# Scan stage: step size from two ScalarE squares, output bias added to the residual by GpSimd

## The chip, the cores and the metric

The kernel runs on one core of one Trainium2 chip. The metric is the device time of one execution in microseconds, the median of several runs. Before the change three runs took 1969.9, 1974.85 and 1976.41 us.

## The reference, cut to what matters

The program is a four-layer network on an activation x of 4 x 512 tokens of 128 features. Each layer does `xn = layernorm(x)` and `x = x + attention(xn) + ffn(xn)`. The change touches only layer 2 (the third one), whose attention is a selective state-space scan and whose ffn is a mixture of 8 experts with top-2 routing:

```python
x_and_res = x @ in_proj_w.T + in_proj_b
x_in = silu(x_and_res[..., :128]); res = x_and_res[..., 128:]
ssm = x_in @ x_proj_w.T + x_proj_b                 # 16 + 128 + 128 columns
delta = clip(softplus(ssm[..., :16] @ dt_proj_w.T + dt_proj_b), 1e-05, 0.1)
Bm, Cm = ssm[..., 16:144], ssm[..., 144:]
A = clip(-exp(A_log), -5.0, -0.01)                 # 128 x 16
# per time step:
h = clip(h * clip(exp(A * delta), 1e-6, 1) + Bm * delta * x_in, -100, 100)
y = sum_over_16(h) * Cm + D_param * x_in
attention = (y * silu(res)) @ out_proj_w.T + out_proj_b
# ffn: hidden = silu(xn @ w_gate.T); sum over 8 experts of combine[:, e] * (hidden @ w_down[e].T)
```

`delta` is the step size. It is softplus of a linear form, clipped at 0.1, so only small values of `exp(z)` matter and `log(1 + exp(z))` can be a short polynomial.

## The kernel before, in words

The kernel runs the layers one after the other; between two blocks of code all engines meet at a barrier. Layer 2 is `norm_and_logits` (layer norm, transposes, router logits) and then `scan_and_ffn`, whose work lies from about 751.7 to 938 us of the trace. The residual x stays in SBUF as 16 tiles of 128 tokens by 128 features (four tiles for each of the four sequences; a sequence is called a batch b here). Small weights are loaded by SyncE's queue during the norm (L3136), among them `b_o`, the output bias, as one row of 4 x 128; every engine waits at the start of the scan block until all of these loads have landed.

The block has a preamble and a loop.

The preamble: TensorE projects the normed input (L1447) into four PSUM banks `m`, ScalarE applies Silu to them (L1554), and TensorE makes the inputs dt, B and C from x_in in one PSUM bank `x` (L1457). VectorE meanwhile does the router: a chain of small operations of 128x128 elements that picks the two best experts (`choose`, L1652 to L1656, L1786 to L1789). After it VectorE makes z, the argument of exp, from the dt bank (`size_input`, L1664), ScalarE exponentiates z in place (`exp_z`, L1568), and VectorE evaluates a polynomial of degree 7 in exp(z) (`log_terms`, L1673, L1676 and five times L1679), and clips it to `delta` (`step_size`, L1683). For batch 0 these steps lie between the steps of the running count of the experts (L1812). GpSimd makes `xd`, `cr`, `xp` and `dr` from delta, x_in and res (L1616 to L1625). ScalarE ends its preamble with the Silus of the other three batches, and then makes the 16 decays `da` of batch 0 (`decays`, L1574 and L1578).

The loop has 4 batches of 16 slots. In slot n of batch b VectorE does, in this order written out by hand: the scan of state n over 512 time steps (L1841), for b < 3 one step of the preparation of batch b+1 (`prepare_slot`), and two weighted sums of an expert's output into x (`weigh`, L1751). In the preparation, slot 1 holds `size_input` (for b+1 of 2 or more), slots 2 to 8 hold one of the seven operations of the polynomial each, slot 9 `step_size`, and slots 11 to 15 the input u of the next scans and a check of its size. Slot 3 also holds `mix` (L1767, y of the batch before from the summed states), and slot 10 `add_out` (L1775, the output product of the batch before added to x). Between two batches VectorE reads a flag and branches (`guard`).

TensorE adds up the 16 states of a batch in PSUM through products with the identity (L1531 and, for a correction, L1535), makes the experts' products four slots ahead (L1479), the next batch's inputs in slots 0, 2 and 5 (L1457), and after slot 6 `out_products`: the bias as a product of a row of ones with `b_o` (L1489, 1 by 512, which also opens the accumulation), four products of `dr` (L1493) and four of `y` (L1497). The last `out_products` stands behind the loop.

What ties the engines: a scan may be four ahead of TensorE's adding (four `h` buffers), four PSUM banks hold the experts' products, and ScalarE's decays have two sets of buffers. SyncE fills memory for layer 3 by DMA during the block.

Of the kernel before, what the change touches and what calls it, by code (L numbers as in the profile page):

```python
# [1315 lines left out]

LOG1P = (1.0, -0.49999995, 0.33332896, -0.24986669, 0.1980376, -0.15143938, 0.0804507)


def scan_tiles(nc, ctx, k, d):  # L1320

    k.s2 = {}
    sources = (("w_in", [P, 2 * P], "s2_w_in"), ("w_dl", [16, P], "s2_w_dl"), ("w_dt", [16, P], "s2_w_dt"),
               ("b_dl", [16, 1], "s2_b_dl"), ("b_dt", [P, 1], "s2_b_dt"), ("b_in", [P, 2], "s2_b_in"),
               ("wg", [P, 2, P], "f2_wg"), ("w_x", [P, 2 * P], "s2_w_bc"), ("b_bc", [P, 2], "s2_b_bc"),
               ("a_log", [P, 16], "s2_a_log"), ("dpar", [P, 1], "s2_dpar"), ("w_o", [P, P], "s2_w_o"),
               ("b_o", [1, 4, P], "s2_b_o"), ("wd", [P, 2, 8, P], "f2_wd"))
    for name, shape, _ in sources:
        k.s2[name] = ctx.enter_context(nc.sbuf_tensor(f"s2_{name}", shape, F32))
    loads = [(k.s2[name], d[src]) for name, _, src in sources]  # L1330
    return loads[:-1], loads[-1]


def scan_and_ffn(nc, k, tag, capacity, band, spare_rows):
# [21 lines left out]
    with ExitStack() as ctx:  # L1356
# [17 lines left out]
        z = ph.sb("z", [P, 2, T])  # L1374
        lp = ph.sb("lp", [P, T])
        delta = ph.sb("delta", [P, 2, T])
        xd = ph.sb("xd", [P, T])
# [26 lines left out]
            "mixed", "cr_ready", "dr_ready", "o_full", "o_read", "link", "size_ready", "top_ready", "table"))  # L1404
        xp_ready = ph.sem("xp_ready")
        lg = k.logits[:, 0:NT * E].rearrange("p (m e) -> p m e", e=E)
# [20 lines left out]
        def _(pe):  # L1427
# [56 lines left out]
            def out_products(b):  # L1484
                if b:
                    pe.wait_ge(o_read, b)
                else:
                    pe.wait_ge(routed, 1)
                pe.matmul(o_ps[:, :], k.ones[0:1, :], b_o[:, :, :].rearrange("a i d -> a (i d)"), start=True, stop=False,  # L1489
                          skip_group_check=True)  # L1490
                pe.wait_ge(dr_ready, b + 1)
                for i in range(QT):
                    pe.matmul(o_ps[:, i * P:(i + 1) * P], dr[:, b % 2, i * P:(i + 1) * P], w_o[:, :], start=False, stop=False,  # L1493
                              skip_group_check=True)
# [47 lines left out]
        def _(act):  # L1542
# [23 lines left out]
            def exp_z(b):  # L1566
                act.wait_ge(z_ready, b + 1)
                act.activation(z[:, b % 2, :], z[:, b % 2, :], ACT.Exp).then_inc(e_ready, 1)  # L1568

            def decays(b):  # L1570
                act.wait_ge(delta_ready, b + 1)
# [3 lines left out]
                for n in range(S):  # L1575
                    if b >= 2 and n == 0:
                        act.wait_ge(scanned, S * (b - 1))
                    act.activation(da[:, b % 2, n, :], delta[:, b % 2, :], ACT.Exp, scale=a[:, n:n + 1]).then_inc(da_ready, 1)  # L1578

# [6 lines left out]
            act.activation(weight[:, 1, :], weight[:, 1, :], ACT.Exp).then_inc(table, 1)  # L1586
            exp_z(0)
            exp_z(1)
            inputs(0)
# [6 lines left out]
            for b in range(1, B):  # L1596
                if b > 1:
                    exp_z(b)
                inputs(b)
                decays(b)  # L1600

        @block.gpsimd
        def _(pool):
            pool.memset(hole[:, :], 1e9).then_inc(hole_set, 1)
            pool.memset(blank[:, :], 0.0).then_inc(hole_set, 1)
            pool.memset(corr[:, 0, :], 0.0).then_inc(corr_zero, 1)
            pool.memset(corr[:, 1, :], 0.0).then_inc(corr_zero, 1)
            pool.wait_ge(k.s2_in, 16 * N_LOADS)
            for b in range(B):
                for name in (("res", b), ("xi", b)):  # L1610
# [20 lines left out]
        def _(v):  # L1631
# [26 lines left out]
            def size_input(b):  # L1658
# [3 lines left out]
                if b >= 2:  # L1662
                    v.wait_ge(delta_ready, b - 1)
                v.tensor_scalar(z[:, b % 2, :], x_ps[:, :], b_fold[:, 0:1], float(np.log(0.2)), ALU.add, ALU.min)\  # L1664
                    .then_inc(x_free, 1)
                v.wait_ge(x_free, i + 1)
                v.sem_inc(z_ready, 1)

            def log_terms(b, n):
                zb = z[:, b % 2, :]  # L1670
                if n == 2:
                    v.wait_ge(e_ready, b + 1)
                    chain(v.tensor_scalar(lp[:, :], zb, LOG1P[6], LOG1P[5], ALU.mult, ALU.add))  # L1673
                elif n == 3:
                    settle()
                    chain(v.tensor_tensor(lp[:, :], lp[:, :], zb, ALU.mult))  # L1676
                else:
                    settle()
                    chain(v.scalar_tensor_tensor(lp[:, :], lp[:, :], LOG1P[8 - n], zb, ALU.add, ALU.mult))  # L1679

# [26 lines left out]
            def prepare_slot(b, n):  # L1707
                if n == 1 and b >= 2:
                    size_input(b)
                if 2 <= n <= 8:  # L1710
                    log_terms(b, n)
                if n == 9:
                    step_size(b)
# [23 lines left out]

            latest = {}
            links = [0]

            def weigh(j):
                p, e = j // 4, j % 4
                for name in fills_of(p):
# [3 lines left out]
                    if e == 0:  # L1747
                        v.wait_ge(m_full[q % NB], q // NB + 1)
                    if tile in latest:
                        v.wait_ge(*latest[tile])  # L1750
                    ins = v.scalar_tensor_tensor(k.x[:, tile, :], m_ps[q % NB][:, e * P:(e + 1) * P],  # L1751
# [17 lines left out]
            def add_out(b):  # L1769
                v.wait_ge(o_full, b + 1)  # L1770
                for tile in range(b * QT, (b + 1) * QT):
                    if tile in latest:
                        v.wait_ge(*latest[tile])
                xs = k.x[:, b * QT:(b + 1) * QT, :]
# [20 lines left out]
            v.tensor_scalar(a[:, :], a[:, :], -1.0, -5.0, ALU.mult, ALU.max).then_inc(a_raw, 1)  # L1795
            log_terms(0, 2)
            v.wait_ge(a_raw, 2)
            v.tensor_scalar(a[:, :], a[:, :], -0.01, None, ALU.min).then_inc(a_raw, 1)
            log_terms(0, 3)
            v.wait_ge(a_raw, 3)  # L1800
            v.tensor_reduce(a_slow[:, :], a[:, :], AX.X, ALU.max).then_inc(a_raw, 1)
            log_terms(0, 4)
            v.wait_ge(both_ready, 1)
            total = v.tensor_copy(before[:, 0, :], both[:, 0, :])
            for i in range(1, NT - 1):
                chain(total)
                if i <= 4:
                    log_terms(0, 4 + i)
                if i == 5:
                    step_size(0)  # L1810
# [1337 lines left out]
def laid_out(a):  # L3148
# [45 lines left out]
    d["s2_w_dt"], d["s2_w_o"] = a["L2_attn_dt_proj_w"].T, a["L2_attn_out_proj_w"].T  # L3194
    d["s2_b_o"], d["s2_b_in"] = np.tile(a["L2_attn_out_proj_b"], (1, 4, 1)), col(a["L2_attn_in_proj_b"], 2)
    xb = a["L2_attn_x_proj_b"]
# [21 lines left out]
```

## Time and profile before

| | us |
|---|---|
| median of 3 runs (lowest, highest) | 1974.85 (1969.9, 1976.41) |
| the profiled execution: its time | 1978.25 |
| its span in the trace | 1976.4 |
| TensorE busy | 1804.1 (91%) |
| VectorE busy | 1469.5 (74%) |
| ScalarE busy | 967.7 (49%) |
| GpSimd busy | 905.5 (46%) |
| granted TensorE clock, mean | 0.951 of full |

The shares are averages over four layers with different limits. The change touches about 186 us of the span, so what counts is which engine sets the pace there. All times below are in us from the span's start; "busy" of TensorE counts overlapping instructions by their modelled ends.

### The profile page before, as it was taken

The numbers are of one execution on the slowest core, as the hardware profiler recorded it, in microseconds if no ns is written. First come the engines' busy times: TensorE is split into PE (matmuls) and PEld (weight loads), VectorE is DVE, ScalarE is ACT, GpSimd is POOL, SyncE is SP. The second block draws the span as 40 slices with busy tenths as digits, with TensorE's granted clock in tenths as the row PEclk, the third lists the DMA queues.
The fourth block names the chain that finished last, engine by engine and source line by source line (L and its number), as shares of the span: only waits on it lengthen the run. The fifth ranks groups of instructions, "written<-read, shape, count | busy, mean of one in ns | idle before, by whom it ended". The sixth has DMA issues, their size and how long they took to land. (4 is left out here: it accounts for less than half of the span.)

```text
span 1976.4 us, 32804 instructions
## 1 busy us (share of the span) xinstructions
PE 1804.1 (91%) x9914; PEld 999.3 (51%) x9914; DVE 1469.5 (74%) x4406; ACT 967.7 (49%) x2260; POOL 905.5 (46%) x1311
## 2 busy tenths in 40 slices
PE   6499997699989948898799999999999999999998
PEld 4233333455546634343466666644455555555544
DVE  6578886677757765998477678568877777777788
ACT  3258785376754426221577777733333333433332
POOL 1637772076633321111277777745444455433441
PEclk9579999699999977999899999999999999999999
DMA  8462223433451029950766566311311342423211
GB/s 285 138 137 33 39 31 65 99 78 106 83 159 29 21 70 160 178 127 0 187 184 166 151 168 182 86 63 46 96 62 62 120 138 84 139 83 102 63 33 33
DMA packets 240592, 201.92 MB, mean 102 GB/s; under 512 B 26883, under 2 KB 223016, under 8 KB 239782
## 3 DMA queue, kind: packets, MB, share of 16 engines
q1 hardware_dynamic: 222614, 171.43, 35.6%
q0 software_dynamic: 17376, 28.29, 5.6%
q8 instruction: 86, 1.41, 0.3%
q14 instruction: 84, 0.69, 0.1%
q10 hardware_dynamic: 432, 0.10, 0.0%
HBM read 116.87 MB, written 82.89 MB: 101 GB/s over the span
## 5 line engine op out<-in xcount | busy, mean ns | idle before, releaser
L2871 DVE SCALAR_TENSOR_TENSOR x<-f_m,f_gs,x 128x128 f32<-128x128 f32 x1024 | 304.8, 343 | 60.4 <-PE f_m L2696 52.9
L515 DVE TENSOR_REDUCE a_nmax<-a_s 128x1 f32<-128x512 f32 (+3 forms) x512 | 276.7, 585 | 83.2 <-PE a_s L321 36.5
L2238 POOL TENSOR_SCALAR a_lg<-a_lg,a_rinv 128x256 f32<-128x256 f32 (+1 forms) x256 | 226.3, 901 | 94.2 <-DVE a_rinv L2275 93.9
L2696 PE MATMUL f_m<-f_wo,f_oT 128*128 128x512 f32 x512 | 248.2, 595 | 0.9
L2644 POOL DMA_INDIRECT f_yg<-yslot,slot x160 | 152.5, 953 | 190.5 <-PE f_s L2730 106.7
L432 ACT ACTIVATE a_pT<-a_st 128x512 f32<-128x512 f32 (+3 forms) x512 | 227.6, 519 | 20.5 <-PE a_st L344 6.6
L318 PE MATMUL a_s<-t_kp,t_qp 96*128 96x512 bf16 (+3 forms) x512 | 166.5, 360 | 12.8 <-DVEq L499 12.6
L341 PE MATMUL a_st<-t_qp,t_kp 99*128 99x512 bf16 (+3 forms) x512 | 163.0, 353 | 2.0 <-ACT a_pT L432 1.2
L2696 PEld LDWEIGHTS f_m<-f_wo,f_oT 128*128 128x128 f32 x512 | 96.0, 190 | 125.6 <-issue 111.2
L2824 ACT COPY f_pT<-f_t 128x512 f32<-128x512 f32 x128 | 75.2, 588 | 167.4 <-PE f_t L2738 127.4
L2871 DVE SCALAR_TENSOR_TENSOR f_val<-f_m,gate,f_val 128x128 f32<-128x128 f32 x336 | 113.2, 343 | 39.7 <-PE f_m L2696 27.4
L2170 ACT ACTIVATE a_lg<-a_lg,a_nmax 128x256 f32<-128x256 f32 (+1 forms) x256 | 120.8, 475 | 31.5 <-DVE a_nmax L2268 31.4
L2730 PE MATMUL f_s<-xn_pair,f_qT 128*128 128x512 f32 x256 | 131.8, 596 | 0.0
L2634 POOL DMA_INDIRECT spare_rows<-xn_pair,slot x96 | 93.0, 969 | 78.5 <-PE f_s L2730 55.9
L442 ACT CAST t_qp<-a_m 3x512 bf16<-3x512 f32 x128 | 74.0, 578 | 102.8 <-PE a_m L329 95.4
L2915 DVE TENSOR_REDUCE f_nmax<-f_s 128x1 f32<-128x512 f32 x128 | 87.4, 683 | 42.5 <-PE f_s L2730 42.4
L2751 PE MATMUL f_o<-f_pT,f_val 128*128 128x512 f32 x256 | 115.2, 593 | 0.0
L2268 DVE CUSTOM_DVE_ANT_0 a_lg<-a_m,a_band 128x256 f32<-128x256 f32 (+1 forms) x256 | 85.0, 384 | 39.1 <-issue 31.9
L356 PE MATMUL a_o<-a_pT,t_vp 128*32 128x512 f32 (+3 forms) x1024 | 108.9, 521 | 0.4 <-DVE a_og L522 0.4
L2634 POOL DMA_INDIRECT rows<-xn_pair,slot x64 | 61.5, 961 | 82.5 <-PE f_s L2730 65.7
L480 POOL DMA_INDIRECT yacc<-a_yc,seat x64 | 85.2, 1332 | 11.2 <-issue 3.4
L2831 ACT ACTIVATE f_prob<-f_s,f_nmax 128x512 f32<-128x512 f32 x128 | 89.1, 696 | 0.8 <-DVE f_nmax L2915 0.5
(428 smaller groups left out, 3757.3 us busy)
## 6 DMA issues: line engine op xcount, KB each, us to landing
a_band<-band SPq DMA_DIRECT2D x64, 512.0 KB, 5.8
band<-s_hole SPq DMA_DIRECT2D x16, 1032.0 KB
band<-a_rows SPq DMA_DIRECT2D x64, 256.0 KB, 5.6
yslot<-f_ys SPq DMA_DIRECT2D x45, 256.0 KB
f_xs<-spare_rows SPq DMA_DIRECT2D x9, 832.0 KB
w_gate_up<-f_wgu_in SPq DMA_DIRECT2D x4, 1536.0 KB, 14.5
t_qp<-parts SPq DMA_DIRECT2D x192, 32.0 KB
t_kp<-parts SPq DMA_DIRECT2D x192, 32.0 KB
```

The costliest lines, as they stand in the source:

```text
L318: last = pe.matmul(ps[:, 0:n], qp[0:MR, h, qt * P:(qt + 1) * P], kp[0:MR, h, 0:n], start=True, stop=not causal)
L341: last = pe.matmul(out[:, q0:T], kp[0:KT, i % H, kt * P:(kt + 1) * P], qp[0:KT, i % H, q0:T], start=True, stop=not causal)
L432: act.activation(pT[:, g % 2, i % 4, begins[kt]:begins[kt] + T - q0], st_ps[w % R][:, q0:T], ACT.Exp).then_inc(exp_done, 1)
L515: v.tensor_reduce(nmax[:, h % 4, qt:qt + 1], s_ps[(b * H * QT + u) % R][:, 0:n], AX.X, ALU.max, negate=True)\
L2170: last = act.activation(lg[:, g % 2, half, p, c0:c0 + w], lg[:, g % 2, half, p, c0:c0 + w], ACT.Exp, bias=nmax[:, g % 2, p, qt:qt + 1], sc ...
L2238: last = pool.tensor_scalar(lg[:, g % 2, half, p, c0:c0 + n], lg[:, g % 2, half, p, c0:c0 + n], rinv[:, g % 2, p, qt:qt + 1], None, ALU.mult)
L2634: pool.indirect_dma_start(rows[n % 3], place_of(c, i, h), k.xn[:, i, :], None).then_inc(sent[n % 3], 16)
L2644: pool.indirect_dma_start(yg[:, n % 2, c, i, :], None, yslot[nth(h) % 3], place_of(c, b * QT + i, h))\
L2696: pe.matmul(ps[:, :], left, w, start=True, stop=True).then_inc(full, 1)
L2730: pe.matmul(s_ps[u % 2][:, :], qT[:, g % 2, qt * P:(qt + 1) * P], tokens(g), start=True, stop=True).then_inc(s_done, 1)
L2751: last = pe.matmul(o_ps[:, :], val[:, g % 3, kt, :], pT[:, g % 2, kt, :], start=(kt == 0), stop=(kt == QT - 1))
L2871: ins = v.scalar_tensor_tensor(out, ps[:, e * P:(e + 1) * P], gate, out, ALU.mult, ALU.add)
```

## The change

The polynomial is written another way. With e = exp(z), before:

```python
LOG1P = (1.0, -0.49999995, 0.33332896, -0.24986669, 0.1980376, -0.15143938, 0.0804507)
```

After, ScalarE makes two shifted squares of e, and VectorE multiplies: lp = (square0 + r0) * e, then (square1 + r1) * lp, a degree 5 polynomial. The cap of z goes from log(0.2) to log(0.106).

The bias is loaded as 128 x 128 (one row for every partition), GpSimd adds it to the residual tiles in four operations of 128x512 at the start of the block, and TensorE's bias product goes. The first write of each x tile waits for that addition.

```diff
+LOG_SCALE = 0.6339928554569843
+LOG_SHIFT = (0.3520040145240758, -0.8358345770896863)
+LOG_REST = (0.8024751436592323, 0.3808488880994126)
...
-               ("b_o", [1, 4, P], "s2_b_o"), ("wd", [P, 2, 8, P], "f2_wd"))
+               ("b_o", [P, P], "s2_b_o"), ("wd", [P, 2, 8, P], "f2_wd"))
...
-                pe.matmul(o_ps[:, :], k.ones[0:1, :], b_o[:, :, :].rearrange("a i d -> a (i d)"), start=True, stop=False,
-                          skip_group_check=True)
                 pe.wait_ge(dr_ready, b + 1)
...
+            def squares(b):
+                if b:
+                    act.wait_ge(delta_ready, b)
+                else:
+                    act.wait_ge(shift_set, 2)
+                act.wait_ge(e_ready, b + 1)
+                for i in range(2):
+                    act.activation(square[:, i, :], z[:, b % 2, :], ACT.Square, bias=shift[:, i:i + 1], scale=LOG_SCALE)\
+                        .then_inc(squared, 1)
...
+                    if b == 0 and n == S // 2:
+                        squares(1)
...
             exp_z(0)
+            squares(0)
             exp_z(1)
...
                     exp_z(b)
+                    squares(b)
...
+            for i in range(2):
+                pool.memset(shift[:, i:i + 1], LOG_SHIFT[i]).then_inc(shift_set, 1)
...
             pool.wait_ge(k.s2_in, 16 * N_LOADS)
+            for b in range(B):
+                xs = k.x[:, b * QT:(b + 1) * QT, :]
+                pool.tensor_tensor(xs, xs, bc(b_o[:, :].unsqueeze(1), [P, QT, P]), ALU.add).then_inc(x_biased, 1)
...
-            def log_terms(b, n):
+            def log_term(b, i):
                 zb = z[:, b % 2, :]
...
+                v.wait_ge(squared, 2 * b + i + 1)
+                if i:
                     settle()
+                chain(v.scalar_tensor_tensor(lp[:, :], square[:, i, :], LOG_REST[i], lp[:, :] if i else zb, ALU.add, ALU.mult))
...
-                if 2 <= n <= 8:
-                    log_terms(b, n)
-                if n == 9:
+                if n in (4, 6):
+                    log_term(b, n // 2 - 2)
+                if n == 8:
                     step_size(b)
...
-            latest = {}
+            latest = {tile: (x_biased, tile // QT + 1) for tile in range(NT)}
```

In the preamble VectorE's seven polynomial operations for batch 0 become two, placed behind the second operation on `a` and in the first step of the running count; `step_size(0)` moves from step 5 of the count to step 3.

## Rows read from the trace of the kernel before

**Rows 1.** Busy time by stretch; columns: us, engines' busy us, TensorE clock, DMA share, GB/s.
```profile
863.50:884.70 21.20, 18.99 (x55) 8.51 (x54) 21.03 (x34) 2.01 (x3) 5.76 (x4) 1.00 0.02 5
823.00:844.20 21.20, 20.75 (x57) 9.43 (x56) 21.05 (x33) 2.01 (x3) 5.76 (x4) 0.95 1.24 182
903.00:933.00 30.00, 28.98 (x78) 12.62 (x76) 28.45 (x50) 0.00 (x0) 5.78 (x3) 1.00 0.00 1
820.00:825.00 5.00, 4.50 (x7) 1.65 (x6) 3.98 (x10) 0.00 (x0) 0.00 (x0) 0.67 1.27 159
```
**Rows 2.** Who waited for whom in the loop, 787 to 938 us.
```profile
DVE s_h L1841 <- PE s_sum L1531: 1.7, 2, 1.0
```
**Rows 3.** The same view in the first half of batch 2, 863.5 to 884.7 us.
```profile
PE s_sum L1531 <- DVE s_h L1841: 2.2, 1, 2.2
```
**Rows 4.** Timeline of VectorE in batch 1: start, duration, line, operation, tiles.
```profile
828.39 0.40 DVE L1673 TENSOR_SCALAR s_lp<-s_z 128x512 f32<-128x512 f32 x1
828.70 0.60 DVE L1751 SCALAR_TENSOR_TENSOR x<-s_m,s_gate,x 128x128 f32<-128x128 f32 x2
...
839.78 0.66 DVE L1679 SCALAR_TENSOR_TENSOR s_lp<-s_lp,s_z 128x512 f32<-128x512 f32 x1
840.37 0.60 DVE L1751 SCALAR_TENSOR_TENSOR x<-s_m,s_gate,x 128x128 f32<-128x128 f32 x2
```
**Rows 5.** Timeline of VectorE where GpSimd is at work, batch 1 and batch 3.
```profile
833.18 1.70 DVE L1679 SCALAR_TENSOR_TENSOR s_lp<-s_lp,s_z 128x512 f32<-128x512 f32 x1
...
836.46 1.75 DVE L1679 SCALAR_TENSOR_TENSOR s_lp<-s_lp,s_z 128x512 f32<-128x512 f32 x1
...
915.80 1.75 DVE L1841 TENSOR_TENSOR_SCAN s_h<-s_da,s_u 128x512 f32<-128x512 f32 x1
917.98 1.21 DVE L1841 TENSOR_TENSOR_SCAN s_h<-s_da,s_u 128x512 f32<-128x512 f32 x1
```
**Rows 6.** Timeline of GpSimd in batches 1 and 3.
```profile
832.28 2.05 POOL L1620 TENSOR_TENSOR s_cr<-s_cm,s_res 128x512 f32<-128x512 f32 x1 [23.44 <-DVE s_y L1767]
...
836.39 1.27 POOL L1625 TENSOR_TENSOR s_dr<-s_xp,s_res 128x512 f32<-128x512 f32 x1
...
915.20 1.27 POOL L1625 TENSOR_TENSOR s_dr<-s_xp,s_res 128x512 f32<-128x512 f32 x1
```
**Rows 7.** Timeline of TensorE and of VectorE at the end of the block.
```profile
933.17 1.12 PE L1489 MATMUL s_o<-s_b_o,ones 1*128 1x512 f32 x2
934.22 1.16 PE L1493 MATMUL s_o<-s_w_o,s_dr 128*128 128x128 f32 x8
...
933.28 0.69 DVE L1767 TENSOR_TENSOR s_y<-s_sum,s_cr 128x512 f32<-128x512 f32 x1 [1.57 <-PE s_sum L1535]
```
**Rows 8.** Timeline of VectorE in the preamble.
```profile
756.94 0.17 DVE L1789 TENSOR_TENSOR s_weight<-s_best 128x16 f32<-128x16 f32 x1
760.27 0.75 DVE L1664 TENSOR_SCALAR s_z<-s_x,s_b_fold 128x512 f32<-128x512 f32 x1 [3.16 <-PE s_x L1457]
...
781.71 1.23 DVE L1697 TENSOR_TENSOR_SCAN s_s<-s_da_slow,s_s 128x512 f32<-128x512 f32 x1 [4.48 <-ACT s_da_slow L1574]
```
**Rows 9.** Timeline of ScalarE in the preamble.
```profile
760.04 1.28 ACT L1583 ACT_TABLE_LOAD   x1
...
763.22 0.63 ACT L1568 ACTIVATE s_z<-s_z 128x512 f32<-128x512 f32 x1 [0.85 <-DVEq L1667]
764.98 0.69 ACT L1560 ACTIVATE s_bm<-s_x,s_b_bc 128x512 f32<-128x512 f32 x1 [1.12 <-PE s_x L1457]
```
**Rows 10.** GpSimd and VectorE in the preamble: the last clearing, then a product and what runs beside it.
```profile
752.52 0.52 POOL L1607 MEMSET s_corr<- 128x512 f32 x1
769.85 1.26 POOL L1616 TENSOR_TENSOR s_xd<-s_delta,s_xi 128x512 f32<-128x512 f32 x1 [16.81 <-DVE s_delta L1683]
...
769.97 1.16 DVE L1812 TENSOR_TENSOR s_before<-s_before,s_both 128x8 bf16<-128x8 bf16 x1
```
**Rows 11.** Timeline of SyncE's queue, the load of the bias row.
```profile
738.88 0.29 SPq L3136 DMA_DIRECT2D s_b_o<-s_b_o_in  x1
```

More of the change, by code:

```diff
@@ L1314, in _ @@
             v.wait_ge(weighed, 2 * NT)
-LOG1P = (1.0, -0.49999995, 0.33332896, -0.24986669, 0.1980376, -0.15143938, 0.0804507)
+LOG_SCALE = 0.6339928554569843
+LOG_SHIFT = (0.3520040145240758, -0.8358345770896863)
+LOG_REST = (0.8024751436592323, 0.3808488880994126)
 def scan_tiles(nc, ctx, k, d):
@@ L1326, in scan_tiles @@
                ("a_log", [P, 16], "s2_a_log"), ("dpar", [P, 1], "s2_dpar"), ("w_o", [P, P], "s2_w_o"),
-               ("b_o", [1, 4, P], "s2_b_o"), ("wd", [P, 2, 8, P], "f2_wd"))
+               ("b_o", [P, P], "s2_b_o"), ("wd", [P, 2, 8, P], "f2_wd"))
     for name, shape, _ in sources:
         k.s2[name] = ctx.enter_context(nc.sbuf_tensor(f"s2_{name}", shape, F32))
-    loads = [(k.s2[name], d[src]) for name, _, src in sources]
+    loads = [(k.s2[name], bc(d[src], [P, P]) if name == "b_o" else d[src]) for name, _, src in sources]
     return loads[:-1], loads[-1]
@@ L1375, in scan_and_ffn @@
         lp = ph.sb("lp", [P, T])
+        square = ph.sb("square", [P, 2, T])
+        shift = ph.sb("shift", [P, 2])
         delta = ph.sb("delta", [P, 2, T])
@@ L1404, in scan_and_ffn @@
             "mixed", "cr_ready", "dr_ready", "o_full", "o_read", "link", "size_ready", "top_ready", "table"))
-        xp_ready = ph.sem("xp_ready")
+        xp_ready, shift_set, squared, x_biased = (ph.sem(s) for s in ("xp_ready", "shift_set", "squared", "x_biased"))
         lg = k.logits[:, 0:NT * E].rearrange("p (m e) -> p m e", e=E)
@@ L1488, in out_products @@
                     pe.wait_ge(routed, 1)
-                pe.matmul(o_ps[:, :], k.ones[0:1, :], b_o[:, :, :].rearrange("a i d -> a (i d)"), start=True, stop=False,
-                          skip_group_check=True)
                 pe.wait_ge(dr_ready, b + 1)
                 for i in range(QT):
-                    pe.matmul(o_ps[:, i * P:(i + 1) * P], dr[:, b % 2, i * P:(i + 1) * P], w_o[:, :], start=False, stop=False,
-                              skip_group_check=True)
+                    pe.matmul(o_ps[:, i * P:(i + 1) * P], dr[:, b % 2, i * P:(i + 1) * P], w_o[:, :], start=(i == 0),
+                              stop=False, skip_group_check=True)
                 pe.wait_ge(mixed, b + 1)
@@ L1663, in size_input @@
                     v.wait_ge(delta_ready, b - 1)
-                v.tensor_scalar(z[:, b % 2, :], x_ps[:, :], b_fold[:, 0:1], float(np.log(0.2)), ALU.add, ALU.min)\
+                v.tensor_scalar(z[:, b % 2, :], x_ps[:, :], b_fold[:, 0:1], float(np.log(0.106)), ALU.add, ALU.min)\
                     .then_inc(x_free, 1)
@@ L1667, in size_input @@
                 v.sem_inc(z_ready, 1)
-            def log_terms(b, n):
+            def log_term(b, i):
                 zb = z[:, b % 2, :]
[L1671 to L1674, printed above, removed]
+                v.wait_ge(squared, 2 * b + i + 1)
+                if i:
                     settle()
[L1676 to L1679, printed above, removed]
+                chain(v.scalar_tensor_tensor(lp[:, :], square[:, i, :], LOG_REST[i], lp[:, :] if i else zb, ALU.add, ALU.mult))
             def step_size(b):
@@ L1748, in weigh @@
                         v.wait_ge(m_full[q % NB], q // NB + 1)
-                    if tile in latest:
-                        v.wait_ge(*latest[tile])
+                    v.wait_ge(*latest[tile])
                     ins = v.scalar_tensor_tensor(k.x[:, tile, :], m_ps[q % NB][:, e * P:(e + 1) * P],
@@ L1771, in add_out @@
                 for tile in range(b * QT, (b + 1) * QT):
-                    if tile in latest:
-                        v.wait_ge(*latest[tile])
+                    v.wait_ge(*latest[tile])
                 xs = k.x[:, b * QT:(b + 1) * QT, :]
@@ L1795, in _ @@
             v.tensor_scalar(a[:, :], a[:, :], -1.0, -5.0, ALU.mult, ALU.max).then_inc(a_raw, 1)
-            log_terms(0, 2)
             v.wait_ge(a_raw, 2)
             v.tensor_scalar(a[:, :], a[:, :], -0.01, None, ALU.min).then_inc(a_raw, 1)
-            log_terms(0, 3)
+            log_term(0, 0)
             v.wait_ge(a_raw, 3)
             v.tensor_reduce(a_slow[:, :], a[:, :], AX.X, ALU.max).then_inc(a_raw, 1)
-            log_terms(0, 4)
             v.wait_ge(both_ready, 1)
@@ L1806, in _ @@
                 chain(total)
-                if i <= 4:
-                    log_terms(0, 4 + i)
-                if i == 5:
+                if i == 1:
+                    log_term(0, 1)
+                if i == 3:
                     step_size(0)
@@ L3194, in laid_out @@
     d["s2_w_dt"], d["s2_w_o"] = a["L2_attn_dt_proj_w"].T, a["L2_attn_out_proj_w"].T
-    d["s2_b_o"], d["s2_b_in"] = np.tile(a["L2_attn_out_proj_b"], (1, 4, 1)), col(a["L2_attn_in_proj_b"], 2)
+    d["s2_b_o"], d["s2_b_in"] = a["L2_attn_out_proj_b"][None], col(a["L2_attn_in_proj_b"], 2)
     xb = a["L2_attn_x_proj_b"]
```

## The prediction

> **What bounds the kernel now.** First I read busy time by stretch inside the block that the change touches. In the loop VectorE has no idle time: 21.03 of 21.20 us in the first half of batch 2, 21.05 of 21.20 in the first half of batch 1 [rows 1]. TensorE is close behind it (18.99 and 20.75 of the same 21.20 us), so the next question is which of the two waits for the other. In the whole loop VectorE's scans waited for TensorE's adding twice, 1.7 us in all [rows 2], and both times at the change of a batch, beside the branch. TensorE in turn sat idle for a scan, 2.2 us at one place in the first half of batch 2 alone [rows 3]. So VectorE sets the pace of the loop, and an operation taken from its list shortens the loop by the time from its start to the start of the next one, not by its printed duration, since neighbours overlap.
>
> The preamble is another matter. VectorE idles 3.16 us before its first z, for TensorE, and 4.48 us before the size check, for ScalarE [rows 8]. The path there goes from z through TensorE's products and ScalarE's Silus to the decays; VectorE's polynomial lies beside it.
>
> Everything behind the block starts at a barrier, so what the block gains the kernel gains.
>
> **The loop.** Start to start, L1673 costs 828.70 - 828.39 = 0.31, and L1679 costs 840.37 - 839.78 = 0.59 [rows 4]; L1676 is like it, with the same inputs, so six are of that kind. Seven operations go: 0.31 + 6 x 0.59 = 3.85. Two come, of the form of L1679 with both inputs in SBUF as before: 1.18. `step_size` only moves. Saved: 2.67 a batch. The preparation of batches 1, 2 and 3 lies in the loop: 3 x 2.67 = 8.0 us.
>
> **The stalls beside GpSimd.** Two of the five L1679 take 1.70 and 1.75 in place of 0.66 [rows 5]; they start while GpSimd's `cr` (832.28 to 834.33) and `dr` (836.39 to 837.66) run [rows 6]. These stalls of 1.04 and 1.09 are no property of the polynomial: they fall on what stands there. After the change slot 4 still holds such an operation, and `cr` still starts right behind `mix`: 1.04 stays. In slot 5 the operation is gone, and `dr` will meet the scan of slot 5 or 6. The row for that is in batch 3, where no polynomial runs: a scan started 0.6 us behind `dr` took 1.75 against 1.21, 0.54 more [rows 5, 6]. So 1.09 becomes 0.54, twice (batches 1 and 2): 1.1 us saved. Bounds: nothing saved, or all four stalls gone, 2 x (1.04 + 1.09) = 4.3. I take the batch 3 row, being the same pair of engines at the same distance.
>
> **The bias product.** It starts at 933.17 and the next product at 934.22 [rows 7]: 1.05 us. In the last `out_products` it runs while VectorE makes y, which ends at 933.28 + 0.69 = 933.97. Without it the four `dr` products end at 933.17 + 1.0 = 934.2, behind y, so the y products and the last addition come 1.05 earlier. The other three lie in the loop beside VectorE: nothing on the path, but 1.05 of relief for TensorE in each first half. `dr` must be there earlier now; behind `mix` it comes 5.6 us later (837.66), while TensorE reaches it only after the adding of slot 6, some 6 us behind `mix` at the earliest. If it should wait, the experts' products and the next adding queue behind it, and the four `h` buffers cover that.
>
> **ScalarE.** Two squares of 128x512 a batch: exp without bias took 0.63, Identity with a bias operand 0.69 [rows 9], so 1.3 for a pair, between 1.2 and 1.4. In the loop ScalarE works 2.01 us in the first 21.2 of a batch [rows 1], and z comes in slot 1 against the use of its square in slot 4: hidden. `squares(1)` stands in the middle of the decays of batch 0 and delays eight decays by 1.3; they are made at 0.62 apart from 781.5 on and used 1.6 and more apart from 787 on: hidden. In the preamble `squares(0)` stands ahead of `exp_z(1)`: exp of batch 0 ends about 762.4, the squares at 763.7, so `exp_z(1)` starts at 763.7 instead of 763.22 and ends at 764.3. Next is the B input at 764.98, which waits for TensorE [rows 9]: 0.65 us of cover are left. VectorE's five saved operations in the preamble are worth nothing, since 4.48 us of idle time already stand behind them [rows 8].
>
> **GpSimd's four additions.** This is the only part that can cost. They start when the clearing ends, 752.52 + 0.52 = 753.04 [rows 10], and two small ones more: about 753.3. One takes 1.26 when undisturbed, as a product of the same shape [rows 10], and 2.05 when disturbed [rows 6]. They run beside the router chain of 13 steps, 0.32 apart, which ends at 756.94 + 0.17 = 757.11 [rows 8]; most of its steps have two SBUF inputs. The rows show what that does: beside `xd` (769.85 to 771.11) a step of the count, also with two SBUF inputs and far smaller, took 1.16, to 771.13 [rows 10]. So each addition lets about one such step through. Four of them run to 753.3 + 4 x 1.26 = 758.3; the chain has got through four blocked steps and one free one by then and has seven left at 0.32 each: 758.3 + 2.3 + 0.15 = 760.8. The first z was due at 760.27 [rows 8]. The 3.16 us of idle time absorb most, and the path slips by 0.5 us. Ends: nothing, if GpSimd is the one that waits; with 2.05 each, 753.3 + 8.2 + 2.45 = 763.95, 3.7 us late. I take 0.5, since the rows at 769.85 have the same engine and the same kind of step.
>
> The Trainium skill ("SBUF — State Buffer", Who interferes with whom) says that a VectorE instruction with two SBUF inputs and a GpSimd instruction that reads SBUF exclude each other, the later one blocking fully until the first is done. The blocked step of 1.16 us agrees [rows 10], and the rule speaks against this change; by it every addition blocks the chain for its whole length, 4 x 1.26 = 5.0 on top of 757.11, thus 762.2 and 1.9 late, which would make the sum 1.4 us smaller. The stretched L1679 of 1.70 agree less: `cr` was stretched too.
>
> **The load.** The bias is now 64 KB in place of 2 KB, issued at 738.88 [rows 11], 12.8 us before the block; it must land by 751.7. Nothing on the path. The first weighing in slot 0 waits for `x_biased`, 758.3 against 788: done.
>
> **The sum.** 8.0 + 1.1 + 1.05 - 0.5 = 9.65 us. The profiled execution took 1978.25 and would take 1968.6; it lay 3.4 above the median of the runs. From the median: 1974.85 - 9.65 = 1965.2.
>
> **The rivals.**
> - *TensorE takes over in the first halves* (chance 0.12). The half of batch 2 shrinks from 21.2 to 21.2 - 2.67 - 0.55 = 18.0. TensorE's work there is 18.99 - 1.05 = 17.9, in batch 1 20.75 - 1.05 = 19.7 [rows 1]. If its 2.2 us of idle time [rows 3] can't be filled, it needs 20.1, twice, and 1.7 more in batch 1 for the low clock: 2 x 2.1 + 1.7 = 5.9 lost, 3.7 gained, 1971.1. Against it: in batch 3 TensorE is busy 28.98 of 30 us [rows 1] and no scan waits, as the buffers reach four slots ahead; and the second halves are loose.
> - *GpSimd's additions run at 2.05* (0.09): slip 3.7 in place of 0.5, gain 6.45, 1968.4.
> - *Square needs a table of its own* (0.05). A load is 1.28 [rows 9]; ahead of the squares and behind them, `exp_z(1)` ends at 764.3 + 2.56 = 766.9, 1.9 behind 764.98. Gain 7.75, 1967.1. In the loop the loads are hidden. Identity follows exp without a load in the trace; Square is not in it. The Trainium skill ("ScalarE: Activation LUTs", Table sets: the hidden batching unit) names cheap functions that are in every set, without Square among them.
> - *The change doesn't reach the total* (0.05): behind the block TensorE sets the pace, and two more dips of its clock there, each like the 5 us at 0.67 from 820 on [rows 1], cost 2 x 2.5: 1970.2.
> - *Slower, by TensorE's clock* (0.05). The granted clock is 0.67 from 820 to 825 [rows 1], when TensorE has been waiting for scans at the end of batch 0, and it is back by 825. While it is at 1.2 GHz instead of 2.4 its work doubles. A dip of d us puts TensorE d/2 behind; some 3 us of buffers cover that. So it costs d/2 - 3, eats the gain from d = 25 us on, and makes the kernel slower by 0.3% from d = 37 on. With 40 us, one batch: 1965.2 + 17 = 1982. Against it: the one dip is under 5 us, and TensorE's gaps get shorter, not longer.
>
> **How the numbers follow.** The forecast has 0.64. Its own range, with the bounds of the stalls and of the slip and the spread of the runs (5 us below the median, 1.6 above), is 1960 to 1968.5. To leave out no more than 0.2 the range goes up to the first rival: 1960.0 to 1971.2. A measurement tells about 0.3%, 5.9 us, from no change, so faster means below 1968.9. The forecast gives 0.61 of its 0.64 to that, GpSimd's slowness 0.05 of 0.09, the table 0.04, TensorE's takeover 0.03: 0.73. Slower is 0.05. The rest is 0.22.
>
> **What would show it.** Right: batches of the loop 3.2 us shorter (40.4 to about 37.2 from the first scan of batch 1 to that of batch 2), no scan waiting for TensorE in slots 4 to 8, VectorE's first z at 760.8, the last y products straight behind `mix`. Wrong: VectorE's waits for TensorE above 1.7 us, a table load beside the squares, a first loop scan later than 788, additions longer than 1.3, or a clock below 1 beyond 825. If the block is shorter by 9 to 10 us and the total is not, the cause lies behind the block.

## The result and the profile after

The changed kernel takes 1962.31 us (median of 14 runs, 1956.99 to 1969.7); the kernel before, on the same chip, 1974.86 (1969.19 to 1977.49). The ratio is 0.9944, 95% interval 0.9933 to 0.9954, that is 9.1 to 13.2 us faster, 11.1 in the middle. 1965.2 was forecast, with a gain of 9.65.

The profiled execution of the changed kernel took 1956.99 us, 21.3 less than that of before. To say where this comes from I cut both traces at the same marks: VectorE's first instruction of the block, the first scan of each batch, the last y (`mix`), the last `add_out`, and the first statistics of layer 3. "Batch" below is from its first scan to that of the next, less the idle time at the branch between them.

| stretch, us | before | changed |
|---|---|---|
| ahead of the block (no edit there but the size of one load) | 751.77 | 743.79 |
| preamble, to the first scan | 35.45 | 33.11 |
| batches 0, 1, 2 | 34.78, 39.10, 39.00 | 32.03, 35.72, 35.73 |
| the three branches | 0.98, 1.44, 0.74 | 1.35, 0.78, 0.44 |
| batch 3, to the last y | 30.02 | 30.03 |
| last y to its addition | 3.03 | 1.94 |
| addition to layer 3 | 2.00 | 2.01 |
| the block | 186.54 | 173.14 |
| layer 3 | 1038.1 | 1037.9 |

So the block is 13.4 us shorter, and 8.0 of the 21.3 lie ahead of it, in code that differs only in the size of the bias load. The block's own difference is what has to be explained.

Busy time of the changed kernel by stretch: the two halves of batch 2, and batch 3; columns as in [rows 1].

```profile
846.80:865.30 18.50, 18.50 (x56) 9.07 (x55) 18.35 (x30) 3.34 (x5) 5.76 (x4) 1.00 0.48 140
865.30:882.90 17.60, 14.93 (x35) 5.87 (x34) 17.14 (x32) 10.52 (x17) 1.28 (x1) 1.00 0.00 0
882.95:912.90 29.95, 28.43 (x78) 12.78 (x77) 28.45 (x50) 0.00 (x0) 5.77 (x3) 1.00 0.00 1
```

VectorE has no idle time in the first half still (18.35 of 18.50), and TensorE, which had 2.2 us [rows 1], has none left either (17.9 busy of 18.0 were forecast). This view can't tell which one holds the other up. The view of who waited for whom in the loop says more; it answers to [rows 2]:

```profile
PE s_sum L1534 <- DVE s_h L1854: 10.1, 14, 1.4
DVE s_h L1854 <- PE s_sum L1534: 2.6, 3, 1.3
DVE x L1790 <- PE s_o L1500: 1.2, 1, 1.2
```

VectorE's three waits, 2.6 us, all stand at the three branches; no scan inside a batch waits. That the view names TensorE there means only that its adding ended last: the scan behind the third branch, at 882.95, needs the buffer of the scan four before it, and TensorE had finished with that by 878.44. So the idle time is that of reading the flag and branching, and it is 3.2 us at the same three places in the kernel before. TensorE still waits for scans, 10.1 us in all.

Timeline of VectorE in batch 1 of the changed kernel, where GpSimd's work meets it, and of GpSimd there (this answers to [rows 4 to 6]):

```profile
818.31 1.22 DVE L1854 TENSOR_TENSOR_SCAN s_h<-s_da,s_u 128x512 f32<-128x512 f32 x1
819.44 1.69 DVE L1696 SCALAR_TENSOR_TENSOR s_lp<-s_square,s_z 128x512 f32<-128x512 f32 x1
821.05 0.60 DVE L1767 SCALAR_TENSOR_TENSOR x<-s_m,s_gate,x 128x128 f32<-128x128 f32 x2
821.57 1.21 DVE L1854 TENSOR_TENSOR_SCAN s_h<-s_da,s_u 128x512 f32<-128x512 f32 x1
822.70 0.58 DVE L1767 SCALAR_TENSOR_TENSOR x<-s_m,s_gate,x 128x128 f32<-128x128 f32 x2
823.20 1.78 DVE L1854 TENSOR_TENSOR_SCAN s_h<-s_da,s_u 128x512 f32<-128x512 f32 x1
824.91 0.66 DVE L1696 SCALAR_TENSOR_TENSOR s_lp<-s_square,s_lp 128x512 f32<-128x512 f32 x1
```

```profile
818.54 2.04 POOL L1642 TENSOR_TENSOR s_cr<-s_cm,s_res 128x512 f32<-128x512 f32 x1 [24.39 <-DVE s_y L1783]
820.56 2.00 POOL L1643 TENSOR_SCALAR s_xp<-s_xi,s_dpar 128x512 f32<-128x512 f32 x1
822.64 1.27 POOL L1647 TENSOR_TENSOR s_dr<-s_xp,s_res 128x512 f32<-128x512 f32 x1
```

The first polynomial operation meets `cr` and takes 1.69 as before; the second is past `dr` and takes 0.66; in its place the scan of slot 6, started 0.56 behind `dr`, takes 1.78 in place of 1.21.

TensorE and VectorE at the end of the block; this answers to [rows 7]. The bias product is gone, and the y products start at 913.72, behind the last `dr` product and right behind y (912.98 + 0.69 = 913.67):

```profile
912.78 1.05 PE L1496 MATMUL s_o<-s_w_o,s_dr 128*128 128x128 f32 x8
913.72 1.16 PE L1500 MATMUL s_o<-s_w_o,s_y 128*128 128x128 f32 x8
...
912.98 0.69 DVE L1783 TENSOR_TENSOR s_y<-s_sum,s_cr 128x512 f32<-128x512 f32 x1 [1.57 <-PE s_sum L1538]
914.92 0.69 DVE L1790 TENSOR_TENSOR x<-s_o,x 128x512 f32<-128x512 f32 x1 [1.25 <-PE s_o L1500]
```

The preamble, GpSimd's additions and the router chain beside them (this answers to [rows 8, 10]), and ScalarE's squares with what follows ([rows 9]):

```profile
745.06 5.09 POOL L1630 TENSOR_TENSOR x<-x,s_b_o 128x512 f32<-128x512 f32 x4
...
745.39 1.08 DVE L1675 TENSOR_TENSOR s_below<-logits,s_best 128x128 f32<-128x128 f32 x1
746.51 1.24 DVE L1676 SCALAR_TENSOR_TENSOR s_below<-s_below,iota 128x128 f32<-128x128 f32 x1
747.78 0.29 DVE L1677 TENSOR_REDUCE s_where<-s_below 128x16 f32<-128x128 f32 x1
748.11 0.92 DVE L1678 TENSOR_TENSOR s_first<-iota,s_where 128x128 f32<-128x128 f32 x1
749.06 1.24 DVE L1801 TENSOR_TENSOR s_ex<-logits,s_best 128x128 f32<-128x128 f32 x1
750.33 0.29 DVE L1802 SCALAR_TENSOR_TENSOR s_left<-s_first,logits 128x128 f32<-128x128 f32 x1
...
752.28 0.17 DVE L1804 TENSOR_TENSOR s_weight<-s_best 128x16 f32<-128x16 f32 x1
753.15 0.75 DVE L1686 TENSOR_SCALAR s_z<-s_x,s_b_fold 128x512 f32<-128x512 f32 x1 [0.69 <-PE s_x L1462]
```

```profile
755.35 1.33 ACT L1580 ACTIVATE s_square<-s_z,s_shift 128x512 f32<-128x512 f32 x2
756.59 0.61 ACT L1571 ACTIVATE s_z<-s_z 128x512 f32<-128x512 f32 x1
757.29 0.69 ACT L1563 ACTIVATE s_bm<-s_x,s_b_bc 128x512 f32<-128x512 f32 x1
```

Four steps of the chain stretch to 0.92 to 1.24, one for each addition; the step that only reads one SBUF tile (L1677) passes at 0.29 beside them, and the chain ends 8.66 us into the block in place of 5.34. No table load stands beside the squares. Yet the first scan comes earlier than before, which no step of the forecast gives. That is the question for the experiments.

### The profile page after: what moved, and what is told of

It is laid out like the page before. It is cut to its first block and busy times, and to the rows that moved or that the text cites. A ratio compares the mean times of both kernels' runs of the same rounds, so it can differ in the third digit from the quotient of the medians.

```text
span 1954.8 us, 32809 instructions
## 1 busy us (share of the span) xinstructions
PE 1788.0 (91%) x9906; PEld 995.1 (51%) x9906; DVE 1460.5 (75%) x4386; ACT 971.4 (50%) x2268; POOL 911.2 (47%) x1317
```

## The experiments

All ratios are against the kernel before on the same chip.

### Which part brings what: e1 and e2

e1 is the changed kernel with TensorE's bias product back and GpSimd's additions gone; e2 is the kernel before with the bias part alone.

```diff
 # e1, against the changed kernel
+                pe.matmul(o_ps[:, :], k.ones[0:1, :], b_o[:, :, :].rearrange("a i d -> a (i d)"), start=True, stop=False,
+                          skip_group_check=True)
...
-                pool.tensor_tensor(xs, xs, bc(b_o[:, :].unsqueeze(1), [P, QT, P]), ALU.add).then_inc(x_biased, 1)
```

> The change without its bias part: the squares and the short polynomial stay, the output bias goes back to TensorE as a product of ones. Block is counted from VectorE's first instruction to the first statistics of layer 3: 186.5 us before, 173.1 changed. My theory (the loop is VectorE's): loop shorter by 9.1 to 10.0 as in the changed kernel, tail not shorter (y to its addition 3.0 us, not 1.9), router chain undisturbed (4.0 us, not 7.3), preamble to the first scan 35.4 if the low TensorE clock near the 10th us of the block belongs to the kernel before, 33 or less if the high clock comes with ScalarE's squares; block 175 to 177.5, total 8.5 to 11.5 faster than before. Rival (the preamble's 2.3 us come from the bias part): preamble 35.4 here and 33.1 in the bias part alone.

> The bias part alone: the polynomial of seven VectorE operations stays. My theory: tail 1.05 shorter; loop unchanged within 0.5 us, since VectorE keeps its list and TensorE's three products less in the loop free nothing; router chain 3.3 longer as in the changed kernel, with a slip of 0.3 to 0.9 of the first z; total 0 to 1 faster, not distinguishable from before. Rival (TensorE also held the loop): the loop shrinks by 1 us or more. Rival (the preamble's 2.3 us come from the bias part): preamble 33.1 and total 3 faster.

e1: 0.994 (0.9919 to 0.9961), so 7.7 to 16.0 us faster. e2: 1.0006 (0.9991 to 1.0021). The time is the polynomial's. In e1 the batches are 32.02, 35.78 and 35.73, as in the changed kernel, and y to addition is 3.03; in e2 they are 34.78, 38.98 and 38.98, as before, and y to addition is 1.94. So taking three bias products from TensorE in the loop frees nothing, and the one in the tail is worth 1.09. Both preambles are long, 35.05 and 35.50. The rival, that the bias part shortened the preamble, falls; and e1 has the squares, so they did not do it either. In e2 the first z waits for the router chain, where in the kernel before it waited for TensorE [rows 8]:

```profile
758.98 0.17 DVE L1790 TENSOR_TENSOR s_weight<-s_best 128x16 f32<-128x16 f32 x1
759.38 0.75 DVE L1665 TENSOR_SCALAR s_z<-s_x,s_b_fold 128x512 f32<-128x512 f32 x1 [0.23 <-DVE s_weight L1790]
```

That is 8.85 us into its block (750.53), against 8.50 before and 8.41 in e1: a slip of 0.35 to 0.44 (0.63 against e3's 8.22, below).

### Where the additions cost: e3 and e7

e3 holds the additions until both z are made. e7 puts four more GpSimd products of the same size between them, on data that nothing uses.

```diff
 # e3
             pool.wait_ge(k.s2_in, 16 * N_LOADS)
+            pool.wait_ge(z_ready, 2)
 # e7
+                pool.wait_ge(extra, b)
+                pool.tensor_tensor(cr[:, :], k.xnT[:, 0:T], k.xnT[:, T:2 * T], ALU.mult).then_inc(extra, 1)
```

> The changed kernel with GpSimd's four additions held until both z are made. My theory: the router chain takes 4.0 us again; the first z stands at 8.5 from the block's start if TensorE is at full clock by then, so 0.3 to 0.9 us against the changed kernel at the most, and the additions meet the running count, which lies beside ScalarE's Silus and costs nothing; total equal to the changed kernel within 1 us. Rival (the additions cost their 3.3 us on the path): 2 us or more faster than the changed kernel.

> The changed kernel with four more GpSimd products of 128x512 between the four additions, on data that nothing uses, so GpSimd works 10.2 us beside the router chain in place of 5.1. My theory (each operation lets about one two-input step of the chain through, and there are only 9 of these in the chain): the chain ends 3 to 4 us later, at about 12 from the block's start in place of 8.7, the cover is used up, and the first z and the first scan stand 3 to 3.5 later; total 3 us slower than the changed kernel. Rival (the cover is deeper, since ScalarE's Silus set the preamble): first scan at most 1 us later.

e3: 0.9942 (0.9919 to 0.9964), not to be told from the changed kernel. Its chain ends at 5.34 again, z stands at 8.22, the first scan at 34.86.

e7: 0.998 (0.9965 to 0.9995), some 7 us slower than the changed kernel, where 3 were expected. The chain ends at 11.79, forecast 12; z slips to 12.02. Eight of its steps are now blocked, one for each operation of GpSimd; three of them, with a step between that passes:

```profile
759.87 1.24 DVE L1806 SCALAR_TENSOR_TENSOR s_left<-s_first,logits 128x128 f32<-128x128 f32 x1
761.14 0.29 DVE L1678 TENSOR_REDUCE s_best<-s_left 128x16 f32<-128x128 f32 x1
761.46 0.92 DVE L1679 TENSOR_TENSOR s_below<-s_left,s_best 128x128 f32<-128x128 f32 x1
762.41 1.24 DVE L1680 SCALAR_TENSOR_TENSOR s_below<-s_below,iota 128x128 f32<-128x128 f32 x1
...
764.95 0.17 DVE L1808 TENSOR_TENSOR s_weight<-s_best 128x16 f32<-128x16 f32 x1
765.35 0.75 DVE L1690 TENSOR_SCALAR s_z<-s_x,s_b_fold 128x512 f32<-128x512 f32 x1 [0.23 <-DVE s_weight L1808]
768.41 0.75 DVE L1690 TENSOR_SCALAR s_z<-s_x,s_b_fold 128x512 f32<-128x512 f32 x1 [2.31 <-PE s_x L1463]
```

The first scan stands at 40.71. Against e4, which has the changed preamble and the same behaviour of the clock (below), 3.1 us of slip in the first z became 4.1 in the second and 5.1 in the first scan, because TensorE worked at 1.2 GHz for longer: its product behind the first z took 2.05 in place of 1.10, and the clock was back at 2.4 GHz only 24 us into the block, in e4 at 18. I had 3 to 3.5. So the cover is about 2.9 us: the 3.16 of idle time less the 0.22 that stand between the chain and z in any case. Four additions lengthen the chain by 3.32, which is 0.4 more than that.

### Does VectorE still set the pace: e4

The second of the two polynomial operations is left out in the loop, so part of the step size of batches 1 to 3 isn't computed (the other one waits for both squares).

```diff
-                if n in (4, 6):
-                    log_term(b, n // 2 - 2)
+                if n == 4:
+                    log_term(b, 0)
```

> The changed kernel with the second of the two polynomial operations left out for batches 1, 2 and 3, so that part of the step size is not computed. My theory (VectorE still sets the pace): 0.59 less in each of three batches, 1.8 us less in the loop than the changed kernel. Rival (TensorE has taken over in the first halves): loop shorter by under 0.6 in all, scans waiting for TensorE's adding in slots 4 to 8.

Batches 31.43, 35.23 and 35.12: 0.60, 0.49 and 0.61 below the changed kernel, 1.7 us in all against 1.8 expected. In the view of waits, VectorE's scans have two waits put down to TensorE's adding, both at branches:

```profile
PE s_sum L1534 <- DVE s_h L1854: 8.5, 13, 1.4
DVE s_h L1854 <- PE s_sum L1534: 1.2, 2, 0.8
```

TensorE has not taken over, though it is busy through the whole first half. The total, 0.9948 (0.9929 to 0.9967), is too coarse to show 1.7 us.

### On what the stall behind mix falls: e6

The two operations move to slots 3 and 7, off the place right behind `mix`.

```diff
-                if n in (4, 6):
-                    log_term(b, n // 2 - 2)
+                if n in (3, 7):
+                    log_term(b, (n - 3) // 4)
```

> The changed kernel with the two polynomial operations in slots 3 and 7 in place of 4 and 6, so that none stands right behind mix, where GpSimd's cr starts. My theory (the stall of 1.0 us falls on the two-input operation that meets cr; a scan that meets GpSimd loses 0.5): batches 1 and 2 show the pattern of batch 3, stalls of 0.5 and 0.5 in place of 1.0 and 0.6, so 0.5 us less in each, 1 us in all. Rival (GpSimd holds VectorE up for as long whatever stands there): batches 1 and 2 as long as in the changed kernel, 36.5 and 36.2.

Batches 32.03, 35.17 and 35.17: 0.55 and 0.56 less in batches 1 and 2. The stalls are now those of batch 3 in the kernel before [rows 5]; the timeline of batch 2, from the polynomial operation in slot 3 on:

```profile
861.36 0.67 DVE L1696 SCALAR_TENSOR_TENSOR s_lp<-s_square,s_z 128x512 f32<-128x512 f32 x1
...
862.47 0.68 DVE L1783 TENSOR_TENSOR s_y<-s_sum,s_cr 128x512 f32<-128x512 f32 x1
863.06 1.21 DVE L1854 TENSOR_TENSOR_SCAN s_h<-s_da,s_u 128x512 f32<-128x512 f32 x1
...
864.70 1.72 DVE L1854 TENSOR_TENSOR_SCAN s_h<-s_da,s_u 128x512 f32<-128x512 f32 x1
...
868.48 1.74 DVE L1854 TENSOR_TENSOR_SCAN s_h<-s_da,s_u 128x512 f32<-128x512 f32 x1
```

The total, 0.9949 (0.9934 to 0.9965), can't show 1.1 us.

Not tried by an edit, but to be read from these traces, is what sets the size of a stall. It is not the kind of instruction: in slot 9 of the changed kernel a scan meets `xd` and loses 0.87, more than any scan beside `cr` or `dr`:

```profile
829.34 1.27 POOL L1638 TENSOR_TENSOR s_xd<-s_delta,s_xi 128x512 f32<-128x512 f32 x1 [4.97 <-DVE s_delta L1700]
829.61 2.08 DVE L1854 TENSOR_TENSOR_SCAN s_h<-s_da,s_u 128x512 f32<-128x512 f32 x1
```

When it starts, `xd` still has 1.00 to run. The same count gives: polynomial operation at 819.44, `cr` has 1.14 left, 1.03 lost; scan at 823.20, `dr` has 0.71 left, 0.57 lost; e6's scans at 864.70 and 868.48, 0.64 and 0.66 left, 0.51 and 0.53 lost. The loss is each time the time that GpSimd's product still has to run, less 0.11 to 0.15. So e6 gains because the next instruction with two SBUF inputs stands 0.5 further behind the start of `cr`, not because it is a scan. Beside `xp`, a `TENSOR_SCALAR` of GpSimd, the scan at 821.57 took 1.21 as ever, and `xp` itself 2.00 in place of the 1.57 that it takes in the preamble.

### The preamble: e5, e9 and e10

The granted clock of TensorE, by stretch, tells the preambles apart. The rows are 5 to 6 us, 6 to 8 us (left out for before, which has 1.00 from 6 us on) and 12 to 18 us into the block; first the kernel before, then the changed one.

```profile
756.77:757.77 1.00, 1.00 (x3) 0.38 (x2) 0.31 (x2) 0.79 (x3) 0.00 (x0) 0.96 1.26 183
763.77:769.77 6.00, 5.13 (x7) 1.85 (x6) 5.66 (x16) 2.63 (x4) 0.00 (x0) 0.50 1.26 182
```

```profile
748.79:749.79 1.00, 1.00 (x2) 0.34 (x1) 0.97 (x2) 0.63 (x2) 1.00 (x2) 0.50 1.47 157
749.79:751.79 2.00, 2.00 (x5) 0.91 (x4) 1.83 (x6) 1.04 (x2) 0.36 (x1) 0.80 1.24 194
755.79:761.79 6.00, 4.76 (x11) 2.08 (x12) 5.50 (x15) 4.60 (x7) 2.47 (x2) 1.00 1.35 180
```

Before, the clock rises to 2.4 GHz near 5 us and is back at 1.2 GHz from 12 to 18 us; in the changed kernel's profile it rises only near 7 us and then stays. Behind the rise TensorE makes single products and waits about 1 us ahead of each (1.01, 1.01 and 0.87 in the kernel before). e5 fills those waits in the changed kernel, e9 in the kernel before, with products whose result is unused, the first of them 8.35 us into the block in e5, behind the rise; e10 is the changed kernel unaltered.

```diff
+                if 1 <= turn[name] <= 3:
+                    pe.matmul(sum_ps[1][:, 0:384], k.ident[:, :], k.xnT[:, 0:384], start=True, stop=True)
                 if turn[name]:
                     pe.wait_ge(x_free, turn[name])
```

> The changed kernel with three idle-time products added on TensorE in the preamble (identity by 384 columns, each ahead of the wait for the x bank, result unused). In five of six profiles so far TensorE's clock rose to 2.4 GHz about 5 us into the block and was at 1.2 GHz again from about 12 to 18.5 us; in the changed kernel's own profile it rose at 7 us and stayed. My theory: that fall belongs to TensorE's gaps around the two z, not to the change. With the gaps filled the clock stays up after its rise, the first loop scan stands at 33.5 or less from the block's start in place of 34.9 to 35.6, and the median is 1.5 to 2.5 us below the changed kernel's. Rival (the fall comes at its own time, whatever TensorE does): clock at 0.5 near the 12th to 18th us again, first scan at 35 or later.

> The kernel before with the three idle-time products of e5 added on TensorE in the preamble, and nothing else. My theory (the fall of TensorE's clock at 12 us into the block belongs to TensorE's gaps, the change has no part in it): the clock stays up after its rise, the first loop scan stands at 33 in place of 35.0 to 35.5, the rest of the block is as in the kernel before: batches of 35.2 to 35.8, 40.0 to 40.5 and 39.7. Total some 2 us below before, near the limit of what can be told. Rival (the change itself holds the clock up, with its squares or additions): clock at 0.5 near the 12th us, first scan at 35.

> The changed kernel once more, unaltered, for another look at the preamble and for its time beside e11 on the same chip. If the clock's rise near 5 us leads to the fall at 12: first scan at 35 to 35.6, block 175 to 175.5; if it rises near 7 us: 33.1 and 173.1. Loop in either case 136.1 from the first scan to the last y, 1.94 from y to its addition. If the preamble of the first profile belonged to the change, it comes out at 33.1 whatever the clock did.

| rise of the clock | kernels | clock at 12 to 18 us | first scan at |
|---|---|---|---|
| early, waits unfilled | before, e1, e2, e3, e4 (e7 apart) | 1.2 GHz | 34.9 to 35.6 |
| late, waits unfilled | changed, e6, e10 | 2.4 GHz | 33.1 to 33.5 |
| late, filled | e9 | 2.4 GHz | 32.9 |
| early, filled | e5, e8, e11 | 2.4 GHz | 32.9, 32.0, 32.0 |

The row that decides is e5's, where the clock rises early (0.92 from 5 to 6 us) and stays:

```profile
756.64:757.64 1.00, 1.00 (x3) 0.38 (x2) 0.97 (x2) 0.74 (x3) 1.00 (x2) 0.92 1.26 160
...
763.64:769.64 6.00, 5.87 (x14) 2.42 (x14) 5.58 (x16) 4.44 (x8) 2.92 (x3) 1.00 1.29 139
```

So the fall belongs to the unfilled waits together with an early rise. Up to the first scan it costs 2.2 to 2.9 us (e4 against the changed kernel's three late rises and e5; e3 against e8; before against e9). e4 has the changed kernel's preamble and fell; so the change doesn't prevent it. And e9 is the kernel before and rose late, ahead of its first added product; so the late rise doesn't need the change, and e9 shows nothing of the filling.

Whether the change makes the late rise likelier stays open: with its preamble (the profiles of after, e4, e5, e6 and e10) the clock rose late in three of five, in the other preambles in one of eight.

The totals of e5, 0.9947 (0.9929 to 0.9965), of e9, 0.9994 (0.998 to 1.0008), and of e10, 0.9948 (0.993 to 0.9967), bear out no gain of 2 us from filling, where e5 was expected 1.5 to 2.5 us below the changed kernel and e9 2 us below the kernel before: where the late rise comes by itself there is less to win, and the runs of each spread over 8 to 13 us.

### All three together: e8 and e11

e8 has e3's wait, e5's products and e6's slots; e11 is the same kernel once more.

> The changed kernel with the additions held until both z are made, the three idle-time products of e5, and the polynomial in slots 3 and 7. If all three theories hold: first z at 8.3, no fall of the clock, first scan at 32.7, batches 1 and 2 0.5 shorter each; 3 to 3.5 us below the changed kernel. If only the loop part holds: 1 us below.

> The kernel of e8 once more. Its block was 170.9 us, 2.2 shorter than the changed kernel's, yet its layer 3 took 1043.5 us against 1037.9, and the total showed no gain. Theory one: layer 3 varies by some 5 us from execution to execution whatever stands ahead of it; then its layer 3 comes out elsewhere between 1038 and 1043 and the median is 1 to 3 us below the changed kernel's. Theory two: what e8 does makes layer 3 longer; then it is at 1043 again and the totals are equal.

The block takes 170.91 and 170.56 us, against 173.14 and 173.25 (e10): 2.2 and 2.7 less: 1.0 to 1.1 from the slots, 1.1 and 1.4 from the preamble, the rest at the branches. The totals: e8 0.9954 (0.9938 to 0.9971); e11 0.9937 (0.9921 to 0.9953) beside e10's 0.9948 on the same chip, medians 1957.55 (e11) and 1960.16 (e10). For e8 3 to 3.5 us below the changed kernel were expected; its total shows none of it. This kernel beats the kernel before; that it beats the changed one shows in the block and isn't settled in the total. Layer 3 took 1043.5 us in e8 and 1037.6 in e11, with the same kernel, so its length varies by itself; nothing shows that e8's came from the edits.

## Why the prediction was right, and where it was off

- **VectorE sets the pace of the loop: right, and shown.** e4 moved the batches by 0.5 to 0.6 for one operation less, and e2 took three products from TensorE for nothing. The rival of TensorE's takeover fell.
- **2.67 us a batch: right, mis-sized by 0.08.** Batch 0, where no stall changes, is 2.75 shorter.
- **The stalls, 0.55 for batches 1 and 2: right in size.** Forecast 3.22 a batch; 3.27 in batch 2, 3.38 in batch 1 of the profile, 3.26 and 3.25 against e2's 38.98. The 1.09 became 0.57, and e6 turned the other 1.04 into 0.5. The row of batch 3 gave the right price because it had the same distance behind `dr` (0.60 against 0.56), as the prediction said; the same pair of engines would not have been enough, as the scan beside `xd` shows with 0.87.
- **The bias product, 1.05: right (1.09),** and nothing in the loop, by e2.
- **GpSimd's additions, 0.5 late: right where the clock rises early.** The first z was forecast at 760.8 - 751.77 = 9.0 into the block and came at 8.85 to 8.89 in e2, e4 and e5, with the chain ending at 8.62 to 8.66. Where the clock rises late, TensorE is itself 0.9 late (first z at 9.3 to 9.5, in e9 without any addition at 9.35) and the additions cost nothing. The upper end, 2.05 an addition, didn't occur: four took 5.09. The Trainium skill's rule ("SBUF — State Buffer", Who interferes with whom), read as the chain losing the whole length of every addition, put the end of the chain at 762.2, 10.4 us into the block; it came at 8.66. The trace agrees with the rule for the single blocked step: the router step at 746.51 met an addition that ran until 747.60 and ended at 747.75. But a step is blocked only for what is left of the addition when it starts: the four lose 0.79, 0.95, 0.63 and 0.95 over their usual 0.29, and these sum to the 3.32 by which the chain is longer, not to 5.1.
- **The squares hidden, no table load: right.** A pair takes 1.33. In the changed kernel's profile `exp_z(1)` ends at 757.20, the product of the B input at 756.15 + 1.10 = 757.25, and the B input starts at 757.29: of the cover of 0.65 next to nothing is left there. In e1, where the clock rose early as in the kernel before, 0.73 is left, and the B input starts 13.2 us into the block in both.
- **Missed: the branches.** They were left at what they were. The third takes 0.74 to 0.78 in all three kernels with the long polynomial and 0.41 to 0.45 in the ten profiles with a short one, 0.3 less. The first two scatter between 0.43 and 1.44, and e10 shows 1.06 at the first where the same kernel had 1.35. Why the third is shorter wasn't tried. The prediction also took the distance from the first scan of batch 1 to that of batch 2 as 40.4; it is 40.54 in the trace, and 36.50 in the changed kernel against the 37.2 given as a sign.
- **Missed in the profile: the preamble.** The forecast had 0.5 more, the profile 2.3 less. The step that failed is that the preamble of one execution was taken for the kernel's: which way the clock goes in it is worth 2 to 3 us. In this profile it happened to go the good way, and that is luck: 2.3 of the block's 13.4 us.
- **Two signs of being wrong that came up and meant nothing.** VectorE's waits put down to TensorE are 2.6 us, above the 1.7 named; they are the branches, whose idle time fell from 3.2 to 2.6. Additions longer than 1.3 us: three took 1.31 to 1.32.
- **TensorE's clock as a danger in the loop: rightly held small.** In the changed kernel's loop the clock is at 1.2 GHz once, for some 3.4 us about the change from batch 0 to batch 1, as before. In e9 it was there for 6.8 us in batch 2, and that batch still took 38.99.

Sum with what the runs show: 2.75 + 3.26 + 3.26 + 0.3 + 1.09 - 0.4 = 10.3, in the measured 9.1 to 13.2, whose middle is 11.1; the forecast said 9.65. What the late rise adds on average isn't known.

## What to carry to other kernels

Where one engine runs without a gap, count an edit start to start on that engine's own timeline, and put a stall next to another engine down to the place, not to the instruction: it passes on to whatever two-input instruction stands there next, and its size here was the time that the other engine's product still had to run. Before moving work to GpSimd beside a VectorE chain with two SBUF inputs, compare the idle time at the end of the chain with one GpSimd duration for each operation as an upper bound (here 0.63 to 0.95 of 1.27 to 1.32 each). And compare two profiles by stretches with the same marks: here 8 of 21 us of difference lay ahead of the block that was changed.

## What the hardware did that I had not expected

- TensorE's clock, once risen, fell back to 1.2 GHz from about 12 to 18 us of the block in all five profiles where it rose early and the waits of 1 us between single products weren't filled (and in e7, there for longer), and in none of the four where it rose late (one of them filled). Three products of 0.8 to 0.9 us in those waits kept it up in three of three early rises.
- The block began between 741.8 and 753.3 us in the profiles of this study, after code that differs at most in the bias load; the same kernel began at 743.8 and 749.0 (the changed one), at 745.5 and 741.8 (e8, e11). A spread of 11.6 us ahead of the edit is as large as what the edit brings, which is why only medians and stretches could be used.
- A VectorE step of 128x16 elements at the start of the block took 1.34 us beside GpSimd's clearing operations, and 0.33 in the kernel before, also beside clearing operations. The long one stands in every profile of a kernel where GpSimd makes the two constants of the squares first, the short one in the three others; why isn't known. It costs nothing, since the router chain starts 1.29 us into the block either way:

```profile
743.79 1.34 DVE L1795 TENSOR_SCALAR s_a_log<-s_a_log 128x16 f32<-128x16 f32 x1 [7.40 <-PEq L61]
```
